# Fused gated cross-attention and expert layer on one core: mask rows picked in SBUF, first loads in another order, and a fourth of the context loaded already turned

## What is computed

```python
def reference(x, ctx_2048, mask_BxS2_bk0, g_xattn, g_ffn, L0_ffn_Wg, L0_ffn_W, L0_ffn_b):
    # x (32, 112, 512), ctx (32, 375, 512), mask (32, 375) bool, Wg (512, 8), W (8, 512, 512), b (8, 512)
    def _L0_xattn_ref(hidden_states, memory_tokens, memory_mask):
        scores = jnp.einsum('bsd,bmd->bsm', hidden_states, memory_tokens) * scale
        scores = jnp.where(memory_mask[:, None, :], scores, neg_inf)
        attn = jax.nn.softmax(scores, axis=-1)
        readout = jnp.einsum('bsm,bmd->bsd', attn, memory_tokens)
        return jnp.where(valid_b[:, None, None], readout, 0)
    def _L0_ffn_ref(x, Wg, W, b):
        probs = jax.nn.softmax(jnp.einsum('bsh,he->bse', x, Wg), axis=-1)
        combine = one_hot(argmax(probs)) * probs
        return jnp.einsum('bsed,bse->bsd', jnp.einsum('bsh,ehd->bsed', x, W) + b, combine)
    x = x + jnp.tanh(g_xattn[0]) * _L0_xattn_ref(_layernorm(x), ctx_2048, mask_BxS2_bk0)
    x = x + jnp.tanh(g_ffn[0]) * _L0_ffn_ref(_layernorm(x), L0_ffn_Wg, L0_ffn_W, L0_ffn_b)
    return x
```

## Time and profile before

| | us |
|---|---|
| three runs | 398.72, 400.95, 399.06; median 399.06 |
| profiled execution | 398.33 |
| its span | 396.4 |
| TensorE busy | 360.9 (91%) |
| VectorE, ScalarE, GpSimd busy | 292.1, 192.8, 223.7 |

### The profile page before, as it was taken

One profiled execution on the slowest core, in us unless ns is written; L12 is line 12 of the kernel. 1 busy time (PEld: TensorE's weight loads), 2 busy tenths in 40 slices (PEclk: granted clock), 3 DMA queues, 4 the chain that ended last, 5 costly groups with the idle time before them and its releaser, 6 DMA issues.

```text
span 396.4 us, 9462 instructions
## 1 busy us (share of the span) xinstructions
PE 360.9 (91%) x2037; PEld 300.4 (76%) x2048; DVE 292.1 (74%) x1089; ACT 192.8 (49%) x453; POOL 223.7 (56%) x456
## 2 busy tenths in 40 slices
PE   0879999999999999999999999668999999999980
PEld 0768888888888888888888877456777777777760
DVE  2467889889889888889889989476775666655540
ACT  2267777777777676777777766221111111111100
POOL 8323656656656665666566554745566555556520
PEclk9999999999999999999999999989999999999996
DMA  6586787778878888889888872325544544444400
GB/s 167 150 207 167 188 221 201 200 210 201 204 218 200 184 225 197 204 194 209 207 213 189 217 198 69 84 54 133 154 143 142 156 138 125 145 145 138 153 30 0
DMA packets 39237, 65.20 MB, mean 164 GB/s; under 512 B 11306, under 2 KB 11918, under 8 KB 39216
## 3 DMA queue, kind: packets, MB, share of 16 engines
q1 hardware_dynamic: 32592, 48.38, 50.6%
q0 software_dynamic: 6624, 16.58, 13.7%
HBM read 49.62 MB, written 17.12 MB: 168 GB/s over the span
## 4 chain that ended last, share of the span: by engine, by line
PE 79%; DMA 7%; DVE 4%; issue 4%; SPq 2%; ACT 1%; POOL 1%; POOLq 0%; DVEq 0%; ACTq 0%
PE read_both L1132 10%; PE ctx_ps L1076 9%; PE read_both L1133 9%; PE score_ps L1171 8%; PE score_ps L1173 8%; PE score_ps L1172 8%; PE score_ps L1101 4%; PE ctx_ps L1153 4%; PE score_ps L1098 3%; PE score_ps L1099 3%; PE score_ps L1100 3%; DMA ctx_sb<-in_ctx 3%; PE prob_ps L1085 3%; DMA ctx_sb<-mid_rows,take 2%; PE prob_ps L1111 2%
## 5 line engine op out<-in xcount | busy, mean ns | idle before, releaser
L646 ACT ACTIVATE ctxT_hi<-ctx_ps 128x512 fp32r<-128x512 f32 x35 | 21.0, 599 | 102.3 <-PE ctx_ps L1153 102.3
L1132 PE MATMUL read_both<-ctx_sb 125*112 125x264 f32 x192 | 61.1, 400 | 2.0 <-DVE lg L828 1.7
L521 POOL DMA_INDIRECT token_list<-pay,pos x32 | 32.3, 1010 | 50.8 <-DVE pos L880 46.1
L1171 PE MATMUL score_ps<-w_hi,ctxT_hi 128*128 x140 | 58.8, 420 | 1.6 <-DVE ctxT_lo L899 1.6
L960 DVE TENSOR_TENSOR ctxT_lo<-ctx_ps,ctxT_hi 128x375 fp32r<-128x375 f32 x96 | 49.4, 542 | 13.2 <-ACT ctxT_hi L638 12.9
L1076 PE MATMUL ctx_ps<-ident,ctx_sb 125*128 125x125 f32 x384 | 54.2, 278 | 3.8 <-DVE ctxT_lo L960 2.1
L1133 PE MATMUL read_both<-ctx_sb 125*112 125x256 f32 x192 | 57.1, 379 | 0.0
L1173 PE MATMUL score_ps<-w_lo,ctxT_hi 128*128 x140 | 55.7, 398 | 0.0
L1172 PE MATMUL score_ps<-w_hi,ctxT_lo 128*128 x140 | 55.1, 394 | 0.0
L591 POOL DMA_INDIRECT ctx_sb<-mid_rows,take x35 | 34.6, 990 | 36.0 <-DVE ctx_sb L918 32.8
L918 DVE SCALAR_TENSOR_TENSOR ctx_sb<-score_ps,li,ctx_sb 128x512 f32<-128x512 f32 x35 | 26.3, 750 | 32.2 <-PE score_ps L1174 23.7
(11 more groups left out here) (143 smaller groups left out, 785.9 us busy)
## 6 DMA issues: line engine op xcount, KB each, us to landing
ctx_sb<-in_ctx SPq DMA_DIRECT2D x32, 672.0 KB
w_raw<-in_L_ffn_W SPq DMA_DIRECT2D x32, 256.0 KB, 5.0
x_sb<-in_x SPq DMA_DIRECT2D x32, 224.0 KB, 4.1
mid_rows<-x SPq DMA_DIRECT2D x32, 224.0 KB, 3.2
ctx_sb<-in_ctx SPq DMA_DIRECT2D x32, 78.0 KB
li<-token_list SPq DMA_DIRECT2D x35, 2.0 KB, 1.8
ctx_sb<-mid_rows,take POOLq DMA_INDIRECT x35, 3.5
out_rows<-ctx_sb,put POOLq DMA_INDIRECT x35, 2.9
```

The source lines that it names most:

```text
L1132: pe.matmul(read_a, turned[:, 0:S], turned[:, S:SE + HALF], start=(c == 0), stop=(c == MC - 1))
L1171: pe.matmul(y_ps[a][:, :], hi, w_hi[:, chunk], start=(k == 0), stop=False)
```

## The change

Four things change.

The **fourth chunk** of every context is also laid out turned in memory as a further input, `in_ctx_turned` (32 x 128 x 375); the columns are in the order in which the transposes leave them. `load_turned` loads 128 rows of 375 floats (192,000 bytes) to a slot of `ctxT_full`, which now has four. The transposes and the copy of chunk 3 go, and the two PSUM banks alternate over batches too, since a batch has three chunks now.

**Mask rows** are picked in SBUF: `mask_add` lies on 128 partitions (those past 32 cleared), and the mask matmul's weights are column j of the identity in bf16, spread over 112 columns, so the product picks row j. No store to memory and no loads of mask rows are left. In the loop the column's address comes from a register.

The **first loads** are reordered: SP begins with batch 0, and its turned chunk; mask, router weights and gates are issued by ScalarE. The turned load of batch i+4 waits on `score_mm` of batch i.

The **first steps** are reordered: TensorE turns context 0 as soon as it is there; the router's sum is one matmul after VectorE has summed the four chunks (`sum_router`), the validity sum and gate come later, GpSimd's `router_constants` stand at step -2 and `late_constants` at step -1 instead of -3.

```diff
+            def load_turned(j):
+                sp.dma_start(ctxT_full[:, j.slot(4), 0:M], ctx_t[bass.ds(j.times(1), 1), :, :].rearrange("o d m -> (o d) m")
+                             ).then_inc(ctxT_ld[j.slot(4)], 16)
...
                 if i.plus(4).within(B):
                     load(i.plus(4))
-                    load_mask(i.plus(4))
+                    sp.wait_ge(score_mm, i.times(1, 1))
+                    load_turned(i.plus(4))
...
-                if at == -3:
+                if at == -2:
+                    router_constants()
+                if at == -1:
                     late_constants()
...
-                act.wait_ge(ctxT_mm, j.times(4, k + 1))
+                act.wait_ge(ctxT_mm, j.times(KS, k + 1))
                 if k == 0 and j.at_least(1):
                     act.wait_ge(score_mm, j.times(1))
-                if k < KS:
-                    act.activation(ctxT_hi[:, k, 0:M], ctx_ps[k % 2][:, 0:M], ACT.Copy).then_inc(ctxT_hi_ok, 1)
-                else:
-                    act.activation(ctxT_full[:, 0:M], ctx_ps[k % 2][:, 0:M], ACT.Copy).then_inc(ctxT_full_ok, 1)
+                act.activation(ctxT_hi[:, k, 0:M], ctx_ps[(j.at + k) % 2][:, 0:M], ACT.Copy).then_inc(ctxT_hi_ok, 1)
...
+            def sum_router():
+
+                dve.wait_ge(wg_ld, 16)
+                dve.tensor_reduce(wg_part[:, :], wg_sb[:, :, :].rearrange("p k e -> p e k"), AX.X, ALU.add).then_inc(wg_part_ok, 1)
...
-                if k >= 2:
+                if k >= 2 or j.at_least(1):
                     pe.wait_ge(ctxT_ok, j.times(KS, k - 1))
-                elif k == 1 and j.at_least(1):
-                    pe.wait_ge(ctxT_full_ok, j.times(1))
-                elif j.at_least(1):
-                    pe.wait_ge(ctxT_ok, j.times(KS))
                 for c in range(MC):
-                    last = pe.transpose(ctx_ps[k % 2][:, c * MP:(c + 1) * MP],
+                    last = pe.transpose(ctx_ps[(j.at + k) % 2][:, c * MP:(c + 1) * MP],
...
-                pe.wait_ge(ctxT_full_ok, j.times(1, 1))
+                pe.wait_ge(ctxT_ld[j.slot(4)], j.rounds(4) * 16 + 16)
...
-                pe.wait_ge(mask_in[j.slot(4)], j.rounds(4) * 16 + 16)
-                pe.matmul(score_ps[a][0:S, 0:M], first_only[:, 0:S], mask_row[:, j.slot(4), :],
+                pe.matmul(score_ps[a][0:SE, 0:MG], xnT_full[:, :], ctxT_full[:, j.slot(4), :], start=False, stop=False)
+                pe.matmul(score_ps[a][0:S, 0:M], ident_bf[:, bass.ds(j.times(1), 1)].to_broadcast([P, S]), mask_add[:, :],
                           start=False, stop=True).then_inc(score_mm, 1)
...
-                    ctx_turn(turned, 3)
```

More of the change, by code:

```diff
@@ L105, in run, with build @@
         body(Count(n))
-def build(nc, x, ctx, mask, g_attn, g_ffn, w_gate, w_exp, b_exp, out):
+def build(nc, x, ctx, ctx_t, mask, g_attn, g_ffn, w_gate, w_exp, b_exp, out):
     B, S, D = x.shape
@@ L283, in build @@
         ctx_ld = [sem(f"ctx_ld{i}") for i in range(4)]
-        mask_in = [sem(f"mask_in{i}") for i in range(4)]
-        fill_st, zero_st, mask_mv, b_mv = sem("fill_st"), sem("zero_st"), sem("mask_mv"), sem("b_mv")
+        ctxT_ld = [sem(f"ctxT_ld{i}") for i in range(4)]
+        fill_st, zero_st, b_mv = sem("fill_st"), sem("zero_st"), sem("b_mv")
         mid_st = [sem(f"mid_st{i}") for i in range(2)]
@@ L522, in file @@
                                         pay[:, j.slot(4), :], None).then_inc(list_st[j.slot(4)], 16)
-            pool.iota(token_ids[:, :], [[S, B]], base=0, channel_multiplier=1).then_inc(const, 1)
-            pool.memset(zeros[:, :], 0.0).then_inc(zero_ok, 1)
-            pool.affine_select(out=before[:, :], in_=ones_bf[:, :], compare_op=ALU.is_gt, fill=0.0, base=0,
-                               pattern=[[1, P]], channel_multiplier=-1).then_inc(const, 1)
-            pool.iota(rev[:, :], [[-1, E]], base=E, channel_multiplier=0,
-                      allow_small_or_imprecise_dtypes=True).then_inc(const, 1)
```

171 lines of the change are left out of this document (93 added, 78 removed).

## The result

| | before | after |
|---|---|---|
| median (4 runs each) | 399.49 us | **411.56 us** |
| lowest, highest | 398.72, 400.95 | 406.36, 412.41 |
| profiled execution, its span | 398.33, 396.4 | 410.73, 408.4 |
| ratio after/before | | 1.027, 95% interval 1.018 to 1.036 |

What follows compares the result with a forecast made beforehand. TensorE was taken to set the attention loop's pace, 7.17 us a period. Start 3.1 us, 27 periods at 0.22 and 0.3 for the last chunk 3 gave 9.3 us off 398.33: 389.0, 390.0 us as median, range 384 to 397.

Steps and rivals of the forecast that it cites:

- Three transposes, 0.32 us each batch: Attention loop, TensorE: dropping three of twelve transposes a batch takes 0.32 us off the period, floor 6.85 us.
- The chain from the turned x to the scores: Loop, ScalarE and VectorE ahead of the scores: TensorE has 0.38 us of room, the edit uses 0.32.
- They straddle the floor: Loop, DMA: a batch's transfers need 6.5 to 7.1 us, on both sides of TensorE's 6.85 us floor.
- T = 6.95: Loop period taken near the scaled DMA share, 6.95 us: 0.22 us gained per period of 7.17.
- Asked for after the context's, so it doesn't hold up its own batch: Loop, SP's queue: the turned load follows the context's and doesn't delay the transposes of its own batch; no cost taken.
- The start: Before batch 4: first scores 5.5 us earlier, of which 3.1 us stay after a wait for context 4.
- fill at 27.0, store at 32.3, context 4 at 38.4: Start, GpSimd and SP: the late fill delays the store of batch 0 and load 4; context 4 lands about 38.4 us.
- First transposes at 6.4: Start, TensorE: x and context of batch 0 all there by 6.4 us, at 238 GB/s; transposes stood at 12.65 before.
- Mask rows in SBUF: Loop, mask matmul with register-addressed weights: 0 to 0.08 us a batch, 0 to 2 us in all; 0 taken.
- The slower rival: Loop loads wait for x2, queue runs dry each batch: 226 GB/s, 7.44 us a period, 403.0 us; chance 0.08.
- the first three: Outcomes counted as faster: the forecast 0.40, TensorE bound with transfer hidden 0.25, that with the whole start 0.08.
- the next two: Rivals: DMA queue takes back the transposes, 395.7 us, chance 0.13; VectorE's chain sets the pace, 394 to 396, 0.06.

Runs made afterwards that it cites:

- e17: Changed kernel with fill and gate early, x and context loads ahead of the store, and the context loaded in two halves; 391.6 us.
- e2: Changed kernel with the turned chunk loaded for batches 0 to 3 only, later chunk 3 neither loaded nor turned; 404.7 us.
- e18: e17 without the turned chunk, chunk 3 turned on TensorE again; 394.6 us.
- e14: Changed kernel with fill and gate early, loads ahead of the store, plus an unawaited 192,000 B memory-to-memory copy a batch; 399.2 us.
- e1: Changed kernel without the turned chunk: chunk 3 turned by TensorE and copied by ScalarE again, mask rows and new start kept; 405.6 us.
- e3: e1 with the turned chunk also loaded from batch 4 on, to a buffer that nobody reads; 409.6 us.
- e5: Changed kernel with the fill, the clearing of the bias rows, and the validity sum and gate moved earlier; 404.7 us.
- e6: e5 without the turned chunk, chunk 3 turned on TensorE again; 399.0 us.
- e13: e6 with x and context of batch i+4 issued ahead of the store of batch i; 399.3 us.

## Why the prediction was wrong, point by point

- **Three transposes, 0.32 us each batch: right in size for a single period, not for the mean.** In e17, where no wait for a context takes their place, most periods are 6.95 us (88.46 to 95.43 is 6.97), between my 6.85 and 7.0. Without the turned load e2 shows a period of 6.85 itself (55.35 to 62.20). The mean of e17 is 7.15, but that of e18, which has the same order and halves and turns the chunk itself, is 7.28: the turned chunk is worth 0.13 a batch, where I took 0.22, and 3.0 us in all by the medians. The chain from the turned x to the scores doesn't hold TensorE up, as read; but another result of VectorE, the chosen expert `hot`, does, for 2.5 us in 7 batches of e17.
- **"They straddle the floor", T = 6.95 in the changed kernel: the step that failed.** I compared bytes with rates, 6.5 to 7.1 us of engine time a batch, and asked no more than whether they fit into a period. The engines had that room: e14 moved 258 GB/s and took no longer. But the loads run in a closed circle (x2, SP, transfer, transposes of four batches later), and the circle took 7.9 to 9.2 us where a period of 6.85 leaves 7.7. Before, it just fitted, with one wait of 0.4 us; the prediction read the share of 0.86 as a seventh of the period to spare. A faster TensorE shortens its own deadline (e2, without the load, still waited, 7.8 to 8.3 us behind x, 8.1 in the mean of 8), and the turned load lengthens the way (after: 8.5 in the mean of the 15 that were waited for). The mean period became 7.59, where the sum took 0.22 off each. That the circle is the limit is shown from its sides, by the bytes added at no cost, by the order and by the halves; a ring with a fifth buffer, the plainest test, wasn't tried.
- **"Asked for after the context's, so it doesn't hold up its own batch": not refuted.** Context 4 was there 9.11 us after the issue of the store ahead of it (36.27 to 45.38) with the turned chunk behind it, and after 9.18 us in e1 (37.44 to 46.62) and 9.20 in e2 (36.54 to 45.74), which load none (9.67 in e3, with the idle load). By 45.38 the engines, nearly empty at 36 us, had moved about 2.2 MB (99 GB/s for 2 us, 277 for 2, 283 for 2, 251 for 3.4), though weights 2, store, x and context are 1.49 MB. e1 moved 2.2 MB too (239 GB/s over its 9.18 us). Whether the load shared the engines with what is issued after it, or the last step of the landing takes up to those 2.7 us (a load of 2 KB takes 1.7 us from issue to landing in the page after), wasn't separated. What the turned load does hold up is the way in the loop, by the 0.4 us between 8.1 and 8.5 above.
- **The start: right in kind, wrong in size.** The step "fill at 27.0, store at 32.3, context 4 at 38.4" was off at each link: VectorE came to x of batch 2 late, so the statistics ended at 24.7 in place of 21.3, the fill was ready at 30.3, the bias rows took 3.07 us of issuing in place of 2.18, the store went at 36.27, and the context landed 9.1 us after it where I had 6.1. In place of 3.1 us gained 3.9 were lost. The wait itself was foreseen at 2 to 4 us and is 3.55. The 38.4 isn't what its own terms give either: 32.3, 2.8 us of issuing and 1.23 MB at 238 to 258 GB/s are 39.9 to 40.3, which would have left 1.2 to 1.6 us of gain in place of 3.1.
- **Two costs that weren't in the sum.** The clock: behind the wait at batch 4 it was granted at 1.2 GHz, and the next period took 9.81 us (45.38 to 55.19), 2.9 above the 6.9 of its periods without a wait; e1 shows the same 2.9 (10.03 after 7.17). The gate: the edit moves `which_valid` behind the x of batch 2 on VectorE, and TensorE waited 2.85 us for it ahead of the second scores; in e5, with the gate early, it waits there too, but 1.38 us and for the context. The sum had nothing for it.
- **First transposes at 6.4: they came at 9.22.** The stretch from 3 to 11 us carried 210 GB/s, not 238, but that explains half a microsecond. As at batch 4, more had moved by then than the sum had: 1.5 MB (161 GB/s over 9.22 us), where x and context 0 are 0.997. With the context in halves (e17) they came at 7.66.
- **Mask rows in SBUF: as costed, nothing.** e6 has them, and in its loop the mean period is 7.32 and most periods 7.17 to 7.26, as before. As a whole e6 and e13 lie within 0.3% of before; that includes the new start, so of its forecast gain of 3.1 us little is seen even when it is repaired.
- **The slower rival** stood at 403.0 with 0.08: "loads wait for x2 and the queue runs dry each batch", at 226 GB/s and 7.44 us. e5, with the start repaired, is almost this case: 226 GB/s, 7.46 us, 404.7. The numbers meet, and so does "loads wait for x2"; but the queue doesn't run dry, for the share is 0.96 there. The prediction gave it a twelfth, and never added up the way from x2 to the landed context.
- **The chances** don't add up to what they say: the first three and two thirds of the next two are 0.86, not 0.84, and 0.06 are left for "same", not 0.08. Nothing hangs on it.

## What to carry to other kernels

Before a faster step is costed, lay the ring's circle beside the period: from the event that frees a buffer to the landed load, against the number of periods that the ring leaves; here one period and a microsecond. If it already fits only just, shortening the work shows little until the load is asked for sooner, split, or put ahead of what nobody waits for, in the order of the deadlines: x, then the context, then the rest. A DMA share near 1 doesn't say that the engines are full. A further transfer that nobody waits for tells more: where it costs nothing, as in e14, they weren't. Where it costs time, as in e3 (4.0 us at 225 GB/s), it may still be the order and not the bytes.
